# Second stage's loads issued in order of need with late waits, and a finish that places 16 token tiles ahead of the other 48 and writes seven groups by rows

## The reference, cut to what matters

```python
mixed = einsum('btd,rde->bte', x, factors) / sqrt(8) + bias      # factors are summed once, weight "f"
q, k, v = x @ Wq, x @ Wk, x @ Wv                                 # rotary, attention in chunks of 128, RMS norm, @ Wo
...
tile_sigs = sign(mean(spline_slopes))                            # 64 tiles of 8 dims
best_cluster = argmax(sign(xf) @ cluster_sigs.T); tile_idx = argmax(tile_scores within best_cluster)
x_slice = take_along_axis(xf, DIMS[tile_idx])                    # 8 values per token
mn, mx = min and max of x_slice over ALL tokens of that tile     # needs every token first
u  = clip((x_slice - mn) / (mx - mn + 1e-8), 0, 1 - 1e-6)
gi = floor(u * 16)
delta = (bases[tile_idx, j, gi] + slopes[tile_idx, j, gi] * (u * 16 - gi)) * output_scale[tile_idx]
out = x; out[token, 8 dims of its tile] += delta
```

## Time and profile before

| | us |
|---|---|
| median of 3 runs (lowest to highest) | 5266.09 (5265.92 to 5266.54) |
| the profiled execution, its own time | 5265.83 |
| its span, first to last instruction | 5264.0 |
| first instruction of the second stage | 3693.0 |
| first instruction of the finish | 5126.5 |
| PE busy over the span | 4829.6 (92%) |
| DVE busy | 4430.6 (84%) |
| POOL busy | 3192.8 (61%) |

### The profile page before, as it was taken

One profiled execution on the slowest core, in us unless ns is written; L12 is line 12 of the kernel. 1 busy time (PEld: TensorE's weight loads), 2 busy tenths in 40 slices (PEclk: granted clock), 3 DMA queues, 4 the chain that ended last, 5 costly groups with the idle time before them and its releaser, 6 DMA issues. The chain is left out here.

```text
span 5264.0 us, 108717 instructions
## 1 busy us (share of the span) xinstructions
PE 4829.6 (92%) x44199; PEld 2786.0 (53%) x44199; DVE 4430.6 (84%) x7283; ACT 2702.7 (51%) x4373; POOL 3192.8 (61%) x1665
## 2 busy tenths in 40 slices
PE   7899999999999999999999999987799999999973
PEld 3444444444444444444444444433588888888862
DVE  4889889898898989889898898987488888888876
ACT  4656666656665666666566666554233333333330
POOL 2676776767767676676767767677234444344436
PEclk9999999999999999999999999998899999999985
DMA  2122222222122221222222222244300000000003
GB/s 103 77 103 75 100 87 89 101 77 105 65 105 95 83 105 73 97 91 87 103 75 101 85 89 101 77 156 181 127 28 26 26 28 26 26 28 26 26 31 70
DMA packets 120079, 415.65 MB, mean 79 GB/s; under 512 B 27040, under 2 KB 28704, under 8 KB 84128
## 3 DMA queue, kind: packets, MB, share of 16 engines
q1 hardware_dynamic: 110336, 397.01, 20.9%
q0 software_dynamic: 7776, 10.67, 0.9%
q10 hardware_dynamic: 1472, 1.04, 0.1%
HBM read 358.68 MB, written 49.99 MB: 78 GB/s over the span
## 5 line engine op out<-in xcount | busy, mean ns | idle before, releaser
L421 POOL TENSOR_TENSOR s<-s,Cb 128x1024 f32<-128x1024 f32 x1024 | 2395.6, 2361 | 968.5 <-DVE state L784 963.2
L779 DVE TENSOR_TENSOR_SCAN s<-s,state,BU 128x512 f32<-128x512 f32 x2048 | 2452.6, 1259 | 350.8 <-PE BU L870 337.0
L613 ACT ACTIVATE s<-dt,ch 128x512 f32<-128x512 f32 x2048 | 1306.9, 715 | 719.3 <-PE Y L887 718.0
L887 PE MATMUL Y<-s,ident 64*64 64x512 f32 x8192 | 1006.5, 607 | 68.6 <-POOL s L421 68.3
L813 PE MATMUL PJ<-xnT,w_in 128*128 128x512 f32 x2048 | 947.2, 606 | 29.6 <-ACT xnT L462 15.0
L870 PEld LDWEIGHTS BU<-spread,dtuT 32*128 32x128 f32 x16384 | 511.9, 188 | 521.1 <-DVE s L779 322.6
L870 PE MATMUL BU<-spread,dtuT 32*128 32x128 f32 x16384 | 609.4, 285 | 138.0 <-DVE s L779 134.9
L813 PEld LDWEIGHTS PJ<-xnT,w_in 128*128 128x128 f32 x2048 | 370.0, 190 | 502.5 <-issue 424.0
L887 PEld LDWEIGHTS Y<-s,ident 64*64 64x64 f32 x8192 | 276.3, 133 | 563.8 <-issue 535.2
L861 PE MATMUL PJ<-w_out,u 128*128 128x512 f32 x960 | 445.7, 607 | 6.9 <-ACT xnT L462 6.4
L658 DVE SCALAR_TENSOR_TENSOR u<-hid,ch,u 128x512 f32<-128x512 f32 x384 | 287.5, 749 | 19.8 <-issue 0.6
(11 more groups left out here) (242 smaller groups left out, 6933.2 us busy)
## 6 DMA issues: line engine op xcount, KB each, us to landing
Cb<-bc SPq DMA_DIRECT2D x256, 1024.0 KB, 4.8
x1t<-x SPq DMA_DIRECT2D x64, 256.0 KB, 2.6
out<-r_t SPq DMA_DIRECT2D x64, 256.0 KB, 2.1
xt<-in_x SPq DMA_DIRECT2D x31, 512.0 KB, 5.4
res<-in_x SPq DMA_DIRECT2D x62, 256.0 KB, 5.2
x<-res SPq DMA_DIRECT2D x62, 256.0 KB, 5.1
w_in<-in_factors SPq DMA_DIRECT2D x5, 1024.0 KB, 7.9
w_parts<-w_in SPq DMA_DIRECT2D x5, 1024.0 KB, 9.0
```

Of the source, the lines that this page charges most:

```text
L421: nc.gpsimd.tensor_tensor(pair, pair, Cb[q % 2][:, 2 * part * T:2 * part * T + 2 * T], ALU.mult).then_inc(z_ready, 1)
L613: nc.scalar.activation(s[k % SLOTS][:, n, :], dt[p % 2][:, gi, :], ACT.Exp, scale=ch[:, 2 * p + gi, 7 + 4 * nq + n:8 + 4 * nq + n]).then_i ...
L779: nc.vector.tensor_tensor_scan(s[k % SLOTS][:, n, :], s[k % SLOTS][:, n, :], BU[:, n::4], state[:, b, k, n:n + 1], ALU.mult, ALU.add).then ...
L887: last_ = nc.tensor.matmul(Y[r][y_rows(r, gi), :], ident[rows, rows], s[(k_even + gi) % SLOTS][rows, n, :], start=False, stop=(n == 3 and ...
```

## The change

**Second stage.** `ident` and `bias_b` get a semaphore of their own (`early_loaded`), `bias_b` moves to the head of ACT's queue, and PE and POOL start on these two. SP's nine late tables and POOL's loads of q, k, v, o wait until "f" has landed. The rest (12 transfers, `w_loaded2`) is waited for by POOL in step 2 and by DVE in step 3. "v" and "o" have separate semaphores. The sign setup moves: DVE and ACT do it at the end of step 1, PE's matmul stands between the products "f" and "q" of step 2 and uses bank 2, the copy ends ACT's step 2, and PE waits for it at the head of step 3.

**Finish.** Tiles are placed in two parts (`PARTS`): 16 tiles first, 48 after group 3. The bounds come by one matmul per pair of tiles, over 128 rows and 6 columns, into bank 6 for the first part and bank 7 for the second. PE's order becomes turns 0 and 1, bounds of the first part, lookups 0 and 1, turns 2 to 7, lookups 2 and 3, bounds of the second part, the other lookups. `BY_ROWS` goes from 5 to 7, so `SCATTERED` from 11 to 9 and the indirect DMAs from 44 to 36.

```diff
@@ SP @@
-            sp.dma_start(ident[:], w["eye"]).then_inc(S["tab_loaded"], 16)
+            sp.dma_start(ident[:], w["eye"]).then_inc(S["early_loaded"], 16)
                     if num(a) == 0:
+                        sp.wait_ge(S["f_loaded"], 32)
                         for dst, src in late:
@@ POOL @@
             load_parts(4, "f", "f_loaded")
-            pool.wait_ge(S["tab_loaded"], 16 * 6)
+            pool.wait_ge(S["f_loaded"], 32)
...
-            pool.wait_ge(S["w_loaded2"], 16 * 13)
+            pool.wait_ge(S["early_loaded"], 16 * 2)
                 a = back(t, 2)
+                    if num(a) == 0:
+                        pool.wait_ge(S["w_loaded2"], 16 * 12)
@@ ACT @@
+            act.dma_start(bias_b[:], w["bias"].to_broadcast([P, HID])).then_inc(S["early_loaded"], 16)
...
-            act.wait_ge(S["setup_dve"], 1)
-            nc.scalar.activation(smean[:], smean[:], ACT.Sign).then_inc(S["setup_act"], 1)
-            act.wait_ge(S["setup_pe"], 1)
-            nc.scalar.copy(sign_b[:], banks[0][:]).then_inc(S["setup_act"], 1)
...
+                if t[1] == 1:
+                    act.wait_ge(S["setup_dve"], 1)
+                    nc.scalar.activation(smean[:], smean[:], ACT.Sign).then_inc(S["setup_act"], 1)
+                if t[1] == 2:
+                    act.wait_ge(S["setup_pe"], 1)
+                    nc.scalar.copy(sign_b[:], banks[2][:]).then_inc(S["setup_act"], 1)
@@ DVE @@
-                    if num(t) == 1:
-                        dve.wait_ge(S["setup_act"], 2)
-                        dve.wait_ge(S["w_loaded2"], 16 * 13)
...
+                    if num(s3) == 0:
+                        dve.wait_ge(S["w_loaded2"], 16 * 12)
                     dve.wait_ge(filled["qT"], num(s3) + 1)
@@ PE @@
-            pe.wait_ge(S["setup_dve"], 2)
-            nc.tensor.matmul(banks[0][:], ones[0:NTILE, :], sdiag...)
-            pe.wait_ge(S["setup_act"], 2)
+            pe.wait_ge(S["early_loaded"], 16 * 2)
...
+                if t[1] == 3:
+                    pe.wait_ge(S["setup_act"], 2)
...
+                if t[1] == 2:
+                    pe.wait_ge(S["setup_dve"], 2)
+                    nc.tensor.matmul(banks[2][:], ones[0:NTILE, :], sdiag...)
@@ finish @@
-    BY_ROWS = 5
+    BY_ROWS = 7
+    FIRST = 4 * N
+    PARTS = (slice(0, FIRST), slice(FIRST, TILES))
@@ DVE @@
+            place(0)
             mark(0)
             for g in range(GROUPS):
-                if g + 1 < GROUPS:
+                if g + 1 < GROUPS and g + 1 != FIRST // N:
                     mark(g + 1)
...
                 pick(g, 1)
+                if g + 1 == FIRST // N:
+                    place(1)
+                    mark(g + 1)
@@ PE @@
+            def bounds(part):
+                at = PARTS[part]
+                for pair in range(at.start // 2, at.stop // 2):
+                    lo = 6 * (pair - at.start // 2)
+                    last_ = nc.tensor.matmul(banks[6 + part][:, lo:lo + 6], ohT(pair), ext[:].rearrange("p r q -> p (r q)"),
+                                             start=True, stop=True)
+                last_.then_inc(ext_full, 1)
...
+            for h in range(FIRST // (2 * N)):
+                turn(h)
...
+            bounds(0)
+            look_up(0)
+            look_up(1)
+            for h in range(FIRST // (2 * N), GROUPS // 2):
+                turn(h)
+            look_up(2)
+            look_up(3)
+            pe.wait_ge(ohT_ready, GROUPS // 2)
+            bounds(1)
+            for g in range(4, GROUPS):
+                look_up(g)
```

More of the change, by code:

```diff
@@ L1514, in body @@
                 if valid(s6):
+                    if num(s6) == 0:
+                        dve.wait_ge(S["setup_act"], 2)
                     score_products(s6)
@@ L1660, in _ @@
         def _(pe):
-            pe.wait_ge(S["setup_dve"], 2)
-            nc.tensor.matmul(banks[0][:], ones[0:NTILE, :], sdiag.rearrange("a i j -> a (i j)"),
-                             start=True, stop=True).then_inc(S["setup_pe"], 1)
-            pe.wait_ge(S["setup_act"], 2)
+            pe.wait_ge(S["early_loaded"], 16 * 2)
             LAG = dict(ffn=1, q=2, k=2, v=2, wo=4)
@@ L1714, in body @@
                     product("ffn", t, xaT, "f")
+                if t[1] == 2:
+                    pe.wait_ge(S["setup_dve"], 2)
+                    nc.tensor.matmul(banks[2][:], ones[0:NTILE, :], sdiag.rearrange("a i j -> a (i j)"),
+                                     start=True, stop=True).then_inc(S["setup_pe"], 1)
                 if valid(s2):
@@ L1887, in _ @@
-            nc.vector.tensor_tensor(rows[:].rearrange("p (t r) -> p t r", r=2), e_q[:, :, :, 2],
-                                    row_base[:].rearrange("p (t r) -> p t r", r=2), ALU.add).then_inc(rows_ready, 1)
-            then(nc.vector.tensor_tensor(by_pair, e_q[:, :, :, 0], e_q[:, :, :, 1], ALU.add))
-            then(nc.vector.tensor_scalar_add(rdn[:], rdn[:], 1e-8))
-            for r in range(2):
-                def half(ap):
-                    return per_dim(ap).rearrange("p (t r) j -> p t r j", r=2)[:, :, r, :]
-                nc.vector.tensor_tensor(half(v16[:]), xs[:].rearrange("p (t r) j -> p t r j", r=2)[:, :, r, :],
-                                        e_q[:, :, r, 1].unsqueeze(2).to_broadcast([P, TILES // 2, DS]), ALU.add)
@@ L1904, in _, with place, dims, spread @@
-            then(nc.vector.tensor_tensor(gf[:], gf[:], gt[:], ALU.subtract))
-            then(nc.vector.tensor_tensor(v16[:], v16[:], gf[:], ALU.subtract))
+            def place(part):
+                at = PARTS[part]
+                n = at.stop - at.start
+                def dims(ap):
+                    return ap[:, at.start * DS:at.stop * DS]
+                def spread(ap):
+                    return ap.unsqueeze(2).to_broadcast([P, n, DS])
+                dve.wait_ge(ext_full, 3 + part)
+                then(nc.vector.tensor_copy(e[:, at, :].rearrange("p t q -> p (t q)"), banks[6 + part][:, 0:3 * n]))
+                nc.vector.tensor_tensor(rows[:, at], e[:, at, 2], row_base[:, at], ALU.add).then_inc(rows_ready, 1)
+                then(nc.vector.tensor_tensor(rdn[:, at], e[:, at, 0], e[:, at, 1], ALU.add))
+                then(nc.vector.tensor_scalar_add(rdn[:, at], rdn[:, at], 1e-8))
+                nc.vector.tensor_tensor(per_dim(dims(v16)), xs[:, at, :], spread(e[:, at, 1]), ALU.add)
+                then(nc.vector.reciprocal(rdn[:, at], rdn[:, at]))
+                then(nc.vector.tensor_tensor(per_dim(dims(v16)), per_dim(dims(v16)), spread(rdn[:, at]), ALU.mult))
+                then(nc.vector.tensor_scalar(dims(v16), dims(v16), 0.0, 1.0 - 1e-6, ALU.max, ALU.min))
+                then(nc.vector.tensor_scalar(dims(v16), dims(v16), float(GRID), None, ALU.mult))
+                then(nc.vector.tensor_copy(dims(gi), dims(v16)))
+                then(nc.vector.tensor_copy(dims(gf), dims(gi)))
+                then(nc.vector.tensor_tensor(dims(gt), dims(gf), dims(v16), ALU.is_gt))
+                then(nc.vector.tensor_tensor(dims(gf), dims(gf), dims(gt), ALU.subtract))
+                then(nc.vector.tensor_tensor(dims(v16), dims(v16), dims(gf), ALU.subtract))
@@ L1989, in _, with turn @@
             nc.tensor.transpose(banks[7][:, 0:P], acc[:].rearrange("p q i -> p (q i)"), ident[:]).then_inc(ext_full, 1)
-            pe.wait_ge(ext_column, 1)
-            for h in range(GROUPS // 2):
+            def turn(h):
                 if h >= 2:
@@ L2026, in _ @@
                 last_.then_inc(looked_up, 1)
+            pe.wait_ge(ext_column, 1)
+            for h in range(FIRST // (2 * N)):
+                turn(h)
+            pe.wait_ge(ext_column, 5)
+            for q in range(2):
+                last_ = nc.tensor.matmul(banks[7][:, P + q:P + q + 1], twice[:, q, :], ext_T[:], start=True, stop=True)
+            last_.then_inc(ext_full, 1)
+            pe.wait_ge(ohT_ready, FIRST // (2 * N))
+            pe.wait_ge(ext_column, 9)
+            bounds(0)
[9 more added lines that the diff above has]
+                look_up(g)
 def constants():
```

81 lines of the change are left out of this document (30 added, 51 removed).

## The result

The changed kernel takes **5235.86 us**, median of 5 runs (5235.28 to 5236.72), beside 5266.09 (5263.25 to 5266.84) for the kernel before in the same comparison: a ratio of 0.9945, 95% interval 0.9932 to 0.9957. It is faster by 30.2 us. Forecast were 36.0, and the measured time lies in the range. The profiled execution took 5235.37 us, its span 5233.6 against 5264.0.

The account below looks back on a forecast made before the run. PE bounds the long middle; the stage's start waits on loads, the finish on PE's bounds, then POOL's indirect DMAs. Start 12.3 - 1.7 - 0.6 = 10.0, finish 19.0 + 14.8 - 7.8 = 26.0: 36.0 off 5265.8 gives 5229.8 us, range 5219 to 5242.

Parts of the forecast that it names:

- So q starts at 3724 and not 3736.3: 12.3 us.: Second stage's start: first "q" product begins 12.3 us earlier, once q and k weights have landed.
- Minus 1.7: Second stage's start: PE has idled by "q", so products at half clock give back 1.7 us (bounds 0 and 5.1).
- minus 0.6: Second stage's start: the sign copy between ACT's copy of `vv` and PE's step 3 gives back 0.6 us.
- That just holds: Second stage's start: `tile_no` lands at 3734.9, in time for POOL's rotary addition at about 3735.
- late tables: Rival, second stage's start: tables land later still and delay POOL's rotary addition by 5 to 8 us: 5235 to 5238; chance 0.14.
- 19.0 us: Finish: everything from the first `mark` to the first indirect DMA moves 19.0 us earlier (17 to 21).
- The term of the bounds: Finish: eight matmuls of two passes, 0.108 to 0.18 us a pass, take 2.1 us; `place(0)` begins 15.5 us earlier.
- 14.8 us: Finish: 36 indirect DMAs instead of 44, each 1.55 + 0.30 us, save 14.8 us if POOL never waits for DVE.
- 7.8 us given back: Finish: DVE's added long instructions (6.6) and `place(1)` (1.2) stop POOL's DMAs, costing 7.8 us; bounds 0 and 11.
- The rival that the long additions do not stop POOL: Finish: the stops would be the row stores, more may cost nothing: 26.0 + 6.6, 5223 us; chance 0.07.
- the likeliest case: Whole kernel: the forecast itself, about 5230 us, within 5224 to 5236; chance 0.60.
- the sum: Whole kernel: start 10.0 plus finish 26.0 make 36.0 us, taken from the profiled 5265.8 us.

Follow-up runs that it names:

- third-tile kernel: Changed kernel with the third token tile loaded at once into r_t[1], ahead of the weights, SP's nine late tables behind it: 5229.89 us, ratio 0.9931.
- the run with five groups: Changed kernel with BY_ROWS = 5 in place of 7, so 44 scatters: 5244.08 us.
- the pieces: Changed kernel with each long spreading and addition of the finish cut into four one-tile pieces, standing between other DVE instructions, mark one group ahead: 5232.9 us, ratio 0.9938.
- finish alone: Changed finish with the second stage of the kernel before: 5240.44 us, ratio 0.9955.
- the start alone: Changed second stage with the finish of the kernel before: 5261.26 us, ratio 0.9992 (interval 0.9983 to 1.0001).
- one reversed list: Start of the kernel before with the changed finish, the nine late tables issued in reverse order, small ones first: 5232.87 us, ratio 0.9941.

## Why the prediction was right, and where it was not

**"So q starts at 3724 and not 3736.3: 12.3 us."** Right. From the stage's first instruction to "q" it was 43.3 us before and is 30.6 now: 12.7. PE waits there 2.23 us for `w_low_k`, a weight, as forecast.

**"Minus 1.7" and "minus 0.6".** This is the step that failed. I took what stands between "q" and PE's step 3 to be PE's own products plus a copy, and looked for a lateness only in the tables. It was 9.3 us before and is 16.6 now: 7.3 given back, not 2.3. The third token tile's load is in none of the sums: it stood at nothing, without a reason. SP issues it when `x_all` frees the buffer, before and after, but now that is 3 us behind the issue of 8 MB of weights. Then comes what the pause leaves behind: PE's clock was at full level at this place before (1.00 from 3745 on, the first row here) and is at half now (0.50, then 0.61), so that from the turn of step 3 (3745.65 before, 3737.75 now) to its product of the masked scores with v it is 20.0 us against 17.4. The first two rows are of the kernel before:

```profile
3745.00:3750.00 5.00, 4.20 (x26) 3.58 (x27) 2.87 (x7) 2.76 (x6) 1.50 (x2) 1.00 0.02 3
3763.07 1.08 PE L1761 MATMUL bank<-scm,vv 128*32 128x128 f32 x32 [0.78 <-DVE scm L1616]
3757.76 1.08 PE L1772 MATMUL bank<-scm,vv 128*32 128x128 f32 x32 [0.78 <-DVE scm L1613]
```

12.7 - 7.3 - 2.6 = 2.8 us, and the stage as a whole shows 3.0. The third-tile kernel gives 5.2 of it back.

**"That just holds", of the late tables.** Right in number and nearly idle in effect: `tile_no` took 24.5 us, was there at 3731.6, and nobody waited for it. It was the next to bind, as the third-tile kernel shows. The rival "late tables", 5235 to 5238, gives the measured time, but by another load than the one it names.

**"19.0 us" to the first scatter.** 17.5. The term of the bounds was mis-sized: 16 passes take 3.55 us, 0.222 each, where I bounded a pass between 0.108 and 0.18; that is 1.5 us. Placing took 3.6 us, half of before, as estimated; the traces show 16 instructions before and 14 now, not the 14 and 13 that I counted, which leaves the term as it is.

**"14.8 us" for eight scatters less.** Right; POOL never waited for DVE, and `place(1)` was hidden. (16 x 1.85 makes 29.6 and not 29.7.) DVE's last addition ended 100.6 us after the finish's start, where I had 97.7, and POOL still closed, at 107.6.

**"7.8 us given back."** 24.2 - 16.1 = 8.1. Two more groups by rows cost 6.8 by the run with five groups (6.6 forecast); `place(1)` cost 0.4 (1.2 forecast); the 0.9 that is left is within what executions of one code differ by. 17.5 + 14.8 - 8.1 = 24.2, of 24.3 measured. The rival that the long additions do not stop POOL is refuted: the stops went when the pieces stood between others or read PSUM, with all row stores still there. The scatters read `delta` and `rows` from SBUF. The Trainium skill ("SBUF — State Buffer", Who interferes with whom) says that a DVE instruction with two SBUF inputs contends with a GpSimd instruction that reads SBUF, and one with at most one SBUF input, outside certain modes, does not; the 57.5 us with one input in PSUM against 80.0 agree. The prediction named only its other sentence, that a two-input addition was not seen to stall a DMA's descriptors; for these scatters the runs speak against it, by nearly all of the 24.2 us. Of the copies and scalar operations in `place(1)`, which the prediction put at up to 1.4 us, one shows: the scatter at 5149.47 starts inside a cast that ends at 5149.72 and ends 1.42 us after it, at a cost of 0.12 us. The others ran beside scatters already under way, and stopped none.

**The total.** The measured 5235.86 us lies 0.14 inside the upper end of the likeliest case, 5224 to 5236, and luck has a part in that: 2.5 of the 30.4 us between the two spans are the first part's, whose code did not change. The parts that the sum speaks of gave 27.9 of its 36.0.

**The execution that the sum starts from.** It had `tile_no` late, and of 38 runs of the kernel before none is as fast as a lucky one would be. In the one lucky execution that was profiled (finish alone) the start of before needs 1424.5 us, less than the 1430.5 of the changed one. Whether the changed start also brought an even time is not shown: five runs of the changed kernel lie within 1.5 us, but eleven of the start alone within 4.2, and fifteen of the kernel before beside them within 7.3.

## What to carry to other kernels

When loads are put in order of need, write down every load that the first steps read, the ones that a freed buffer releases included: a 256 KB tile issued 3 us behind 8 MB of weights arrives with the last of them, and a 0.5 KB table does too. Where the writing order leaves it free, issue the small things first; one reversed list took 7.5 us off the profiled second stage, the whole new order 3.0. Beside a stream of indirect DMAs, keep VectorE's instructions with both inputs in SBUF from standing in a row, or give them one input in PSUM, before paying for the balance between the two engines.

## What the runs showed of the hardware

- A scatter that starts while VectorE is in an unbroken run of instructions with two SBUF inputs ends 1.42 us after that run (8.46 us for one instead of 1.55), however the run is cut; a gap of 0.10 us between two instructions ends the run. The scatter at 5174.59, under way when the spreading began at 5174.85, took its 1.55 us. With one input in PSUM, 5 us of the same work stop none.
- Beside full DMA queues a 0.5 KB load took 7.9, 11.7, 24.5 or 25.2 us; 11.7 and 25.2 are the same code in two executions.
- A matmul pass of 128 rows and 6 columns took 0.222 us, two of 64 rows and 3 columns 0.108 each; at a granted clock of 0.50 both times, joining two halves into one pass saved PE nothing.
- In the third-tile kernel two pauses of PE of 1.16 and 0.92 us came before a granted clock of 0.69; with the first alone it stayed at 1.00.
